# Writing out the last step of an attention loop, and storing each projected block once

## The chip, the cores and the metric

The kernel runs on one core of a Trainium2 chip. The metric is the device time of one execution in microseconds; the kernel before took 5323.51 us, the median of three runs that went from 5317.22 to 5327.42 us.

## The reference, cut to what matters

A two-layer hybrid network on `x` of shape (16, 512, 128) in float32: sixteen sequences of 512 tokens. Three of its stages are attentions with 16 heads of width 8:

```python
x = x + L0_attn_a(layernorm(x))   # causal, with a relative position bias per head
x = x + ffn(layernorm(x)); x = x + mamba(layernorm(x)); x = x + ffn(layernorm(x))
x = x + L1_attn_a(layernorm(x))   # not causal; keys and values from a latent of width 32
x = x + experts(layernorm(x))
x = x + L1_attn_b(layernorm(x))   # causal, q and k rotated by position
x = x + experts(layernorm(x))
# each attention:
scores = einsum('bhqd,bhkd->bhqk', q, k) / sqrt(8)  (+ bias, + mask)
out    = einsum('bhqk,bhkd->bhqd', softmax(scores), v) @ Wo
```

## The kernel before, in words

`program` runs the stages one after another; each is one or more phases, and at the end of a phase all engines meet in a barrier (`Phase.__exit__`, L58). An attention is a phase `project` and a phase `attend`; in the first one a short phase that lays out the relative bias stands between them. Below they are called a0 (bias, causal), a1 (not causal) and b1 (causal).

`project` goes over NB = 16 blocks of 512 tokens, one per sequence. TensorE, ScalarE, VectorE and GpSimd make q and k, each split into bf16 parts that add up to the float32 value, and v. SyncE (SP) then stores the block to DRAM: `store(n, u)` issues seven DMAs, six to the two `stack` tensors (L1068) and one to `values` (L1069), 1.75 MB in all. The DRAM tensors have NB + 1 blocks. After the sixteen blocks SP issues a seventeenth, `store(NB, ...)`, which writes the last block's data once more into place NB; at the end it waits for all stores.

`attend` works in groups of four heads: four groups to a sequence, 64 groups in all. Each group passes through a software pipeline whose stages are spread over steps. In step n the engines do, for the same instant of time:

- `scores_t` of group n (TensorE, L1302, with mask and bias matmuls L1320 and L1312): transposed scores into the three PSUM banks of `t_ps`; ScalarE turns each tile into `probs` with an exponential (L1428). In a0 VectorE first adds the bias to the first tile of each pair (L1476).
- `scores_s` of group n + 3 (TensorE, L1271) into the three banks of `s_ps`, of which VectorE takes the row maxima (`maxima`, L1462 when causal, L1465 when not). These are only for the shift of the softmax.
- `mt` of group n + 2 (TensorE, L1347), `shift_high` and `shift_low` (VectorE, L1488, L1494): the maxima are transposed, negated and split in two; SP stores them (`store_m`) and loads them back as extra rows of `t_q` (`load_t`).
- `pv` of group n - 1 (L1333), after which ScalarE copies `o_ps` to `o_sb` (L1414, once per group, near the start of a step), and `ot` of group n - 2 (L1354), with a reciprocal and a division on VectorE. Once per sequence come `bt` (L1360, with the copy `gather`) and `wo` (L1365, with the addition to x).

SP loads q and k of group n + 4 for the maxima (`load_s`) and those of group n + 1 for the transposed scores (`load_t`). Order on each engine is the order of the code; engines wait for each other on counting semaphores. `FIRST` and `USES` list the uses of the PSUM bank `misc`, so that each can wait for the one before by number.

The loop over sequences: b = 0 is written out; then TensorE, ScalarE and VectorE run `Fori(0, 15 // UNROLL)`, whose body holds UNROLL sequences. UNROLL is 1 in the causal attentions (12 tiles of a group divide by the ring of 3 banks) and 3 in a1 (16 tiles don't). So the loop has 15 turns of four steps in a0 and b1, and 5 turns of twelve steps in a1. No step asks whether group n + 3 still exists: in the last sequence (steps 60 to 63) the loads, scores and maxima of groups 64 to 67, a sequence past the end, are done on the extra DRAM block, and nothing uses them. After the loop a tail finishes `pv`, `ot`, `bt` and `wo` of the last groups.

Of the kernel before, what the change touches and what calls it, by code (L numbers as in the profile page):

```python
# [16 lines left out]
F32 = mybir.dt.float32  # L17
BF16 = mybir.dt.bfloat16
# [6 lines left out]
P = 128  # L25
NB = 16
T = 512
# [840 lines left out]
def project(core, x, stacks, v_dram, w):  # L868
# [10 lines left out]
    with core.phase() as ph:  # L879
# [180 lines left out]
        @block.sync  # L1060
        def _(sp):
            def store(n, u):
                for first, count in STEPS:
                    for s in range(2):
                        dst = stacks[s][n, :, first:first + count]
                        src = (parts[:, Q_PARTS[first], 0, u].unsqueeze(1).to_broadcast([P, count, T]) if s == 0
                               else parts[:, 0:count, 1, u])
                        sp.dma_start(dst, src).then_inc(stored[u], 16)  # L1068
                sp.dma_start(v_dram[n].rearrange("p c g d -> p (c g d)"), v_sb[:, u].rearrange("p c d -> p (c d)")  # L1069
                             ).then_inc(stored[u], 16)  # L1070

            for n in range(NB):
                sp.wait_ge(v_ready, n + 1)
                sp.wait_ge(middle_ready, 2 * n + 2)
                sp.wait_ge(low_ready, 2 * n + 2)
                store(n, n % PB)
            store(NB, (NB - 1) % PB)
            for u in range(PB):
                sp.wait_ge(stored[u], 16 * STORES * ((NB - 1 - u) // PB + 1 + (u == (NB - 1) % PB)))


def attend(core, x, stacks, v_dram, shift_dram, w, scale, causal, bias=None):
# [36 lines left out]
    with core.phase() as ph:  # L1119
# [38 lines left out]
        LEAD = 2  # L1158

        def use_no(b, g, what):  # L1160
            if isinstance(b, int) and b == 0:
                return LEAD + FIRST.index((g, what))
            return LEAD + len(FIRST) + len(USES) * (b - 1) + USES.index((g, what))

        def spread(b, k):

# [3 lines left out]
        def _(sp):  # L1170
# [43 lines left out]

            def step(b, g):
                n = 4 * b + g
                sp.wait_ge(s_mm, 2 * NTILE * (n + 2) + 2 * NTILE)
                load_s(b, g + 4)
                if not (isinstance(b, int) and n == 0):
                    sp.wait_ge(t_mm, USES_OF_GROUP * n)  # L1220
                sp.wait_ge(v_ready, n + 1 + 1)
                load_t(b, g + 1)
                store_m(use_no(b, g, "MT"), b, g + 2)

            for g in range(4):
                step(0, g)
            with sp.Fori(1, NB) as b:
                for g in range(4):
                    step(b, g)

            sp.wait_ge(s_loaded[0], 64 * 34)
            sp.wait_ge(s_loaded[1], 64 * 34)
            sp.wait_ge(t_loaded[0], 96 * 33)
            sp.wait_ge(t_loaded[1], 96 * 32)
            sp.wait_ge(v_loaded[0], 16 * 33)
            sp.wait_ge(m_stored[0], 16 * 33)
            sp.wait_ge(m_stored[1], 16 * 33)

        @block.gpsimd
        def _(pool):  # L1240
# [17 lines left out]
        def _(pe):  # L1258
# [114 lines left out]
            def step(b, v, g):  # L1373
                started = 4 * b + g if isinstance(b, int) else 99
                for pair, i in itertools.product(range(2), range(NTILE)):
                    at = NTILE * pair + i
                    scores_t(b, v, g, pair, i)
                    scores_s(b, v, g + AHEAD, pair, i)
                    if pv_pieces[at] and started >= 1:
                        pv(b, g - 1, *pv_pieces[at]) if g else pv(b - 1, 3, *pv_pieces[at])  # L1380
                    if at == misc_at["MT"]:
# [24 lines left out]
        def _(act):  # L1406
# [28 lines left out]
            for g in range(4):  # L1435
                step(0, 0, g)
            with act.Fori(0, (NB - 1) // UNROLL) as turn:
                for u in range(UNROLL):
                    for g in range(4):
                        step(UNROLL * turn + (1 + u), 1 + u, g)  # L1440
            last = use_no(NB, 0, "MT")
            evacuate(NB - 1, 2, use_no(NB - 1, 3, "OT"))
            evacuate(NB - 1, 3, last)

# [1 line left out]
        def _(dve):  # L1446
# [81 lines left out]
            def step(b, v, g):  # L1528
                started = 4 * b + g if isinstance(b, int) else 99
                for pair, i in itertools.product(range(2), range(NTILE)):  # L1530
                    at = NTILE * pair + i
                    if i in ADDED:
                        add_bias(b, v, g, pair, i)
                    maxima(b, v, g + AHEAD, pair, i)
                    if at == misc_at["MT"]:
                        shift_high(use_no(b, g, "MT"), b, g + 2)
                    if at == misc_at["MT"] + 1:
# [10 lines left out]
            for g in range(4):  # L1548
                step(0, 0, g)
            with dve.Fori(0, (NB - 1) // UNROLL) as turn:  # L1550
                for u in range(UNROLL):
                    for g in range(4):
                        step(UNROLL * turn + (1 + u), 1 + u, g)
            last = use_no(NB, 0, "MT")
            for k in (2, 3):
                sums_inverted(last + k - 2)
                divide(NB - 1, k)
# [639 lines left out]
def program(nc, a, out, phases=PHASES):  # L2197
    with ExitStack() as ctx:
# [13 lines left out]
        stacks = [nc.dram_tensor(f"stack_{s}", [NB + 1, P, PLACES, T], BF16).ap() for s in "qk"]  # L2212
        shift_dram = nc.dram_tensor("shifts", [NB + 1, HEADS, 4, SHIFT_ROWS, P], BF16).ap()
        v_dram = nc.dram_tensor("values", [NB + 1, P, 4, 4, 32], F32).ap()
# [184 lines left out]
```

## Time and profile before

| what | us |
|---|---|
| median of 3 runs | 5323.51 |
| the profiled execution | 5320.46 |
| its span, first to last instruction | 5318.7 |
| a0: project ends, attend runs | about 146, then 202 to 1004 |
| a1: project ends, attend runs | about 2636, then 2637 to 3440 |
| b1: project ends, attend runs | about 4133, then 4134 to 4756 |

Busy over the whole span: TensorE 78%, VectorE 67%, ScalarE 54%, GpSimd 30%. These are means over stages of different kinds; what the change touches lies in the three attentions, which take some 2250 us. Times in the rows below are microseconds from the start of the span.

### The profile page before, as it was taken

To read this page: it belongs to the slowest core of one execution; us is meant where nothing else is said; L and a number is where in the kernel's file an instruction comes from. 1 tells how busy PE (TensorE), PEld (TensorE's weight loads), DVE (VectorE), ACT (ScalarE), POOL (GpSimd) and SP (SyncE) were. 2 spreads that over 40 slices of the span, in tenths; PEclk is the share of its full clock that TensorE was granted. 3 is DMA by queue.
4 is the path that set the end of the run, shared out by engine and by line. 5 is a ranking of instruction groups with operands and counts; after the bars stand their busy time and mean duration, and the time that the engine had idled before them with its cause. 6 is when DMAs were issued, how large, how long until landed. Compare 5 with 4: busy or idle time off the path is not lost. (4 is left out here: it accounts for less than half of the span.)

```text
span 5318.7 us, 109649 instructions
## 1 busy us (share of the span) xinstructions
PE 4172.8 (78%) x31637; PEld 2106.4 (40%) x31638; DVE 3541.8 (67%) x8801; ACT 2850.0 (54%) x5331; POOL 1612.8 (30%) x1559
## 2 busy tenths in 40 slices
PE   6499999898667677778789999933987699983598
PEld 3144444552222222226222222323983244442497
DVE  3388888647899998984499999831116788873012
ACT  7255555676555555556667777721325466662232
POOL 3000000011777777741200000055536000006552
PEclk9699999999899998999889999966999799995799
DMA  7522222106100010000722222213665333321466
GB/s 257 150 73 72 74 76 72 33 0 216 42 26 26 26 36 28 26 13 2 244 73 74 78 76 75 72 38 123 214 189 209 108 95 96 98 77 46 142 212 191
DMA packets 546193, 502.03 MB, mean 94 GB/s; under 512 B 163774, under 2 KB 482911, under 8 KB 545788
## 3 DMA queue, kind: packets, MB, share of 16 engines
q1 hardware_dynamic: 527724, 460.95, 29.2%
q0 software_dynamic: 18160, 37.42, 2.1%
q8 instruction: 137, 2.24, 0.2%
q14 instruction: 172, 1.41, 0.1%
HBM read 330.57 MB, written 167.58 MB: 94 GB/s over the span
## 5 line engine op out<-in xcount | busy, mean ns | idle before, releaser
L1428 ACT ACTIVATE p_probs<-p_t_ps 128x512 f32<-128x512 f32 (+1 forms) x2304 | 1141.8, 551 | 680.9 <-PE p_t_ps L1320 243.8
L1963 PE MATMUL p_y_ps<-p_prod,c_ident 128*128 128x512 f32 x1024 | 554.5, 667 | 295.5 <-DVE p_prod L2148 290.9
L1333 PE MATMUL p_o_ps<-p_probs,p_v_st 128*32 128x256 f32 (+3 forms) x8704 | 727.0, 407 | 3.2 <-ACT p_o_sb L1414 2.9
L1465 DVE TENSOR_REDUCE p_row_max<-p_s_ps 128x1 f32<-128x512 f32 x1072 | 669.0, 680 | 71.9 <-PE p_s_ps L1271 55.6
L1254 POOL TENSOR_TENSOR p_v_st<-p_v_raw,p_ones 128x128 f32<-128x128 f32 x192 | 87.5, 456 | 2068.4 <-PE p_o_ps L1333 1946.9
L2097 POOL TENSOR_TENSOR p_dbx<-p_dtx,p_b_sb 128x512 f32<-128x512 f32 x512 | 632.4, 1267 | 113.2 <-ACT p_b_sb L1994 112.4
L2139 DVE TENSOR_TENSOR_SCAN p_state<-p_da,p_dbx 128x512 f32<-128x512 f32 x512 | 598.8, 1208 | 84.6 <-ACT p_da L2032 67.0
L1302 PE MATMUL p_t_ps<-p_t_q,p_t_k 50*128 50x512 bf16 (+3 forms) x3072 | 516.4, 336 | 147.6 <-ACT p_probs L1428 58.6
L1271 PE MATMUL p_s_ps<-p_s_k,p_s_q 48*128 48x512 bf16 (+3 forms) x3216 | 508.6, 340 | 146.8 <-DMA p_s_k<-stack_k 75.0
L1462 DVE CUSTOM_DVE_ANT_0 p_tried<-p_s_ps,p_s_bias 128x512 bf16<-128x512 f32 (+3 forms) x1072 | 470.5, 485 | 137.0 <-PE p_s_ps L1271 134.4
L1462 DVE CUSTOM_DVE_ANT_0 p_tried<-p_s_ps,c_mask_row 128x512 bf16<-128x512 f32 (+3 forms) x1072 | 470.5, 485 | 86.2 <-PE p_s_ps L1271 76.2
L791 DVE TENSOR_TENSOR p_y<-p_out_ps,p_raw 128x256 f32<-128x256 f32 x142 | 60.3, 425 | 581.3 <-PE p_out_ps L742 581.3
L1963 PEld LDWEIGHTS p_y_ps<-p_prod,c_ident 128*128 128x128 f32 x1024 | 188.7, 202 | 556.9 <-DVE p_prod L2148 478.3
L1994 ACT ACTIVATE p_b_sb<-p_b_ps 128x512 f32<-128x512 f32 x256 | 152.6, 596 | 430.2 <-PE p_b_ps L1932 419.4
L1302 PEld LDWEIGHTS p_t_ps<-p_t_q,p_t_k 50*128 50x128 bf16 x3072 | 149.1, 93 | 563.6 <-ACT p_probs L1428 361.5
L803 POOL DMA_INDIRECT weighed_rows<-p_y,p_raw x284 | 273.1, 962 | 296.9 <-DVE p_y L791 252.4
L2032 ACT ACTIVATE p_da<-p_dt,p_rate 128x512 f32<-128x512 f32 x512 | 337.4, 686 | 29.5 <-DVE p_state L2139 28.6
L773 ACT ACTIVATE p_hidden<-p_hid_ps 128x512 f32<-128x512 f32 x284 | 169.6, 597 | 316.0 <-PE p_hid_ps L731 313.7
L2148 DVE TENSOR_TENSOR p_prod<-p_state,p_c_ps 128x512 f32<-128x512 f32 x512 | 322.3, 670 | 0.0
L1312 PE MATMUL p_t_ps<-p_bias_parts,c_flip 64*128 64x384 bf16 (+2 forms) x4608 | 302.8, 269 | 0.0
L654 POOL DMA_INDIRECT routed_rows<-p_rows,p_index x256 | 249.2, 974 | 163.3 <-DVEq L599 86.5
L1333 PEld LDWEIGHTS p_o_ps<-p_probs,p_v_st 128*32 128x32 f32 x8704 | 174.7, 108 | 262.0 <-issue 245.4
(256 smaller groups left out, 6888.0 us busy)
## 6 DMA issues: line engine op xcount, KB each, us to landing
p_wb<-in_w SPq DMA_DIRECT2D x142, 512.0 KB
p_s_q<-stack_q SPq DMA_DIRECT2D x408, 96.0 KB
p_s_k<-stack_k SPq DMA_DIRECT2D x408, 96.0 KB
p_t_q<-stack_q SPq DMA_DIRECT2D x390, 96.0 KB
p_t_k<-stack_k SPq DMA_DIRECT2D x390, 96.0 KB
mamba_inputs<-p_out SPq DMA_DIRECT2D x17, 1536.0 KB, 5.7
p_inp<-mamba_inputs SPq DMA_DIRECT2D x17, 1536.0 KB
stack_q<-p_parts SPq DMA_DIRECT2D x51, 384.0 KB
```

The source lines that it names most:

```text
L1271: mm = pe.matmul(s_ps[:, banks[r], at:at + width], s_q[rows, g % 2, pair, c * P:(c + 1) * P], s_k[rows, g % 2, pair, 0:width], start=True, ...
L1302: mm = pe.matmul(out[r], t_k[rows, g % 2, pair, c * P:(c + 1) * P], t_q[rows, g % 2, pair, first:first + width], start=True, stop=not mask ...
L1312: mm = pe.matmul(out[r], bias["flip"][rows, k], bias["t"][q][rows, k, 2 * g + pair, first - c * P:first - c * P + width], start=False, sto ...
L1333: mm = pe.matmul(o_ps[32 * j:32 * j + 32, at:to], v_st[:, g % 2, c, j, :], probs[:, g % 2, j, place[c] + at - first:place[c] + to - first] ...
L1428: act.activation(exps, tile, ACT.Exp, scale=scale).then_inc(expd, 1)
L1462: read = dve.tensor_tensor_reduce(tried[:, slot, at:at + width], scores, over, 1.0, LOWEST, ALU.add, ALU.max, found)
L1465: read = dve.tensor_reduce(found, scores, X, ALU.max)
L1963: pe.matmul(y_ps[:, h], w["ident"], prod[:, k_slot(n, h, RS)], start=(n == 0), stop=(n == STATE - 1)).then_inc(acc_mm, 1)
L2032: act.activation(da[:, k_slot(n, h, RA)], dt[:, u, h], ACT.Exp, scale=rate[:, h, n:n + 1]).then_inc(da_ready, 1)
L2097: pool.tensor_tensor(dbx[:, k_slot(n, h)], dtx[:, u, h], b_sb[:, n % RB], ALU.mult).then_inc(dbx_ready, 1)
L2139: dve.tensor_tensor_scan(out=state[:, out], data0=da[:, k_slot(n, h, RA)], data1=dbx[:, s], initial=0.0, op0=ALU.mult, op1=ALU.add).then_i ...
L2148: dve.tensor_tensor(prod[:, s], state[:, s], c_ps[:, n % 2], ALU.mult).then_inc(prod_ready, 1)
```

## The change

`project`: the seventeenth store is gone, and with it its part of the final wait; the DRAM tensors have NB blocks instead of NB + 1.

`attend`: the last sequence is written out behind the loop, on TensorE, ScalarE, VectorE and SP (GpSimd keeps its loop over all 16). In the written-out copy `exists(b, k)` is known, and work on groups 64 and later is left out: `load_s` in all four steps, `scores_s` and `maxima` in steps 61 to 63, `mt` with its two shifts and its store in steps 62 and 63, `load_t` in step 63. For the loop to divide by UNROLL, it begins at sequence `FROM` = UNROLL: in a1 sequences 0, 1 and 2 are written out in front of it (before, only 0), the loop has 4 turns of three sequences instead of 5, and sequence 15 follows. In a0 and b1 the loop has 14 turns instead of 15.

```diff
-            store(NB, (NB - 1) % PB)
             for u in range(PB):
-                sp.wait_ge(stored[u], 16 * STORES * ((NB - 1 - u) // PB + 1 + (u == (NB - 1) % PB)))
+                sp.wait_ge(stored[u], 16 * STORES * ((NB - 1 - u) // PB + 1))
...
+    FROM, TO = UNROLL, NB - 1
+    GROUPS = 4 * NB
...
+        LAST = [use for use in USES if use not in ((2, "MT"), (3, "MT"))]
...
+        def exists(b, k):
+            return not isinstance(b, int) or 4 * b + k < GROUPS
...
             def step(b, g):
                 n = 4 * b + g
-                sp.wait_ge(s_mm, 2 * NTILE * (n + 2) + 2 * NTILE)
-                load_s(b, g + 4)
...
+                if exists(b, g + 4):
+                    sp.wait_ge(s_mm, 2 * NTILE * (n + 2) + 2 * NTILE)
+                    load_s(b, g + 4)
+                if exists(b, g + 1):
...
+                    load_t(b, g + 1)
+                if exists(b, g + 2):
+                    store_m(use_no(b, g, "MT"), b, g + 2)
...
-                    scores_s(b, v, g + AHEAD, pair, i)
+                    if exists(b, g + AHEAD):
+                        scores_s(b, v, g + AHEAD, pair, i)
...
-            for g in range(4):
-                step(0, 0, g)
-            with pe.Fori(0, (NB - 1) // UNROLL) as turn:
+            for b in range(FROM):
+                for g in range(4):
+                    step(b, b, g)
+            with pe.Fori(0, (TO - FROM) // UNROLL) as turn:
                 for u in range(UNROLL):
                     for g in range(4):
-                        step(UNROLL * turn + (1 + u), 1 + u, g)
-            last = use_no(NB, 0, "MT")
+                        step(UNROLL * turn + (FROM + u), FROM + u, g)
+            for g in range(4):
+                step(TO, TO, g)
+            last = END_USE
```

ScalarE and VectorE get the same loop as TensorE, `maxima` and the two shifts the same conditions; the numbers in `use_no` follow `LAST` in the last sequence.

## Rows read from the trace of the kernel before

**Rows 1.** SP's DMA issues at the end of project a0, then a1, then b1.

```profile
137.19 0.44 SPq L1069 DMA_DIRECT2D values<-p_v_sb  x1
142.52 0.45 SPq L1069 DMA_DIRECT2D values<-p_v_sb  x1
...
2627.67 0.45 SPq L1069 DMA_DIRECT2D values<-p_v_sb  x1
...
2632.97 0.45 SPq L1069 DMA_DIRECT2D values<-p_v_sb  x1
...
4124.89 0.46 SPq L1069 DMA_DIRECT2D values<-p_v_sb  x1
...
4130.23 0.44 SPq L1069 DMA_DIRECT2D values<-p_v_sb  x1
```

**Rows 2.** Window: from:to, length, PE, PEld, DVE, ACT, POOL busy, clock, DMA, GB/s.

```profile
2610.00:2634.00 24.00, 5.75 (x24) 2.86 (x23) 3.80 (x6) 7.95 (x15) 6.79 (x6) 0.66 1.00 345
```

**Rows 3.** GpSimd's first work in attend a1, with its idle time before.

```profile
2636.78 1.80 POOL L1242 MEMSET p_t_k<- 128x2048 bf16 x1 [16.57 <-POOLq L58]
```

**Rows 4.** Windows in a1: two ordinary steps; the same two around the first, last back-jump.

```profile
2806.07:2827.83 21.76, 20.45 (x186) 5.96 (x186) 21.27 (x42) 18.13 (x35) 0.91 (x2) 1.00 0.31 81
2850.95:2880.41 29.46, 23.86 (x186) 6.21 (x186) 21.64 (x42) 18.13 (x35) 0.91 (x2) 0.83 0.23 62
3277.24:3305.37 28.13, 22.60 (x186) 6.07 (x186) 21.46 (x42) 18.14 (x36) 0.91 (x2) 0.88 0.25 65
```

**Rows 5.** Weight loads behind the first back-jump; TensorE's waits, 2700 to 3430: total, times, longest.

```profile
2864.57 0.11 PEld L1302 LDWEIGHTS p_t_ps<-p_t_q,p_t_k 50*128 50x128 bf16 x2 [4.04 <-issue]
...
PE p_t_ps L1302 <- issue: 13.5, 4, 3.6
```

**Rows 6.** DMA queues between 340 and 990 (loop of a0): packets, MB, share.

```profile
q1 hardware_dynamic: 82028, 47.79, 27.3%
```

**Rows 7.** Windows over the first and the second turn of a0's loop.

```profile
284.53:332.53 48.00, 43.94 (x606) 22.45 (x604) 41.80 (x164) 24.96 (x54) 1.82 (x4) 1.00 0.28 77
332.53:380.00 47.47, 43.93 (x606) 22.37 (x604) 41.81 (x164) 24.96 (x53) 1.82 (x4) 1.00 0.27 72
```

**Rows 8.** Windows over steps 61 to 63 (eviction to eviction) of a0, a1, b1.

```profile
960.79:995.22 34.43, 32.21 (x445) 16.41 (x441) 30.09 (x120) 18.07 (x40) 0.91 (x2) 1.00 0.26 70
3395.33:3428.65 33.32, 31.60 (x281) 9.32 (x281) 32.10 (x62) 26.60 (x51) 0.91 (x2) 1.00 0.28 78
4719.62:4746.15 26.53, 24.36 (x325) 10.79 (x325) 23.76 (x107) 17.51 (x39) 0.91 (x2) 1.00 0.36 96
```

**Rows 9.** The same windows, instructions on `s_ps` alone: PE, PEld, DVE busy.

```profile
960.79:995.22 34.43, 5.88 (x46) 2.00 (x46) 20.73 (x48) 1.00 0.26 70
3395.33:3428.65 33.32, 8.89 (x46) 2.23 (x46) 29.08 (x48) 1.00 0.28 78
4719.62:4746.15 26.53, 5.92 (x46) 1.85 (x46) 20.39 (x47) 1.00 0.36 96
```

**Rows 10.** TensorE's weight loads in order, step 63 of a1, with idle before.

```profile
3418.61 0.10 PEld L1302 LDWEIGHTS p_t_ps<-p_t_q,p_t_k 50*128 50x128 bf16 x2 [0.54 <-ACT p_probs L1428]
3419.17 0.10 PEld L1271 LDWEIGHTS p_s_ps<-p_s_k,p_s_q 48*128 48x128 bf16 x2 [0.47 <-DVE p_row_max L1465]
3419.49 0.16 PEld L1333 LDWEIGHTS p_o_ps<-p_probs,p_v_st 128*32 128x32 f32 x8 [0.23 <-issue]
3420.49 0.09 PEld L1347 LDWEIGHTS p_misc<-c_ident,p_row_max 128*16 128x16 f32 x1 [0.84 <-DVE p_row_max L1465]
3420.69 0.10 PEld L1302 LDWEIGHTS p_t_ps<-p_t_q,p_t_k 50*128 50x128 bf16 x2
```

**Rows 11.** Weight loads' waits over steps 61 to 63 of a1: total, times, longest.

```profile
PEld p_t_ps L1302 <- ACT p_probs L1428: 7.3, 15, 1.0
...
PEld p_s_ps L1271 <- DVE p_row_max L1465: 4.2, 15, 0.5
PEld p_misc L1347 <- DVE p_row_max L1465: 2.5, 3, 0.8
```

More of the change, by code:

```diff
@@ L1162, in use_no @@
                 return LEAD + FIRST.index((g, what))
-            return LEAD + len(FIRST) + len(USES) * (b - 1) + USES.index((g, what))
+            uses = LAST if isinstance(b, int) and b == NB - 1 else USES
+            return LEAD + len(FIRST) + len(USES) * (b - 1) + uses.index((g, what))
+        def exists(b, k):
+            return not isinstance(b, int) or 4 * b + k < GROUPS
         def spread(b, k):
@@ L1216, in step @@
                 n = 4 * b + g
-                sp.wait_ge(s_mm, 2 * NTILE * (n + 2) + 2 * NTILE)
-                load_s(b, g + 4)
[L1219 to L1223, printed above, removed]
+                if exists(b, g + 4):
+                    sp.wait_ge(s_mm, 2 * NTILE * (n + 2) + 2 * NTILE)
+                    load_s(b, g + 4)
+                if exists(b, g + 1):
+                    if not (isinstance(b, int) and n == 0):
+                        sp.wait_ge(t_mm, USES_OF_GROUP * n)
+                    sp.wait_ge(v_ready, n + 1 + 1)
+                    load_t(b, g + 1)
+                if exists(b, g + 2):
+                    store_m(use_no(b, g, "MT"), b, g + 2)
             for g in range(4):
                 step(0, g)
-            with sp.Fori(1, NB) as b:
+            with sp.Fori(1, TO) as b:
                 for g in range(4):
                     step(b, g)
[L1231 to L1237, printed above, removed]
+            for g in range(4):
+                step(TO, g)
+            for u in range(2):
+                sp.wait_ge(s_loaded[u], 64 * (GROUPS // 2))
+                sp.wait_ge(t_loaded[u], 96 * (GROUPS // 2))
+                sp.wait_ge(v_loaded[u], 16 * (GROUPS // 2))
+                sp.wait_ge(m_stored[u], 16 * (GROUPS // 2))
         @block.gpsimd
@@ L1388, in step @@
                         bt(use_no(b, g, "BT"))
[L1390 to L1392 removed]
+            for b in range(FROM):
+                for g in range(4):
+                    step(b, b, g)
+            with pe.Fori(0, (TO - FROM) // UNROLL) as turn:
                 for u in range(UNROLL):
                     for g in range(4):
[L1395 to L1396 removed]
+                        step(UNROLL * turn + (FROM + u), FROM + u, g)
+            for g in range(4):
+                step(TO, TO, g)
+            last = END_USE
             for piece in pv_pieces:
@@ L1433, in step @@
                         evacuate(b, g - 2, before) if g >= 2 else evacuate(b - 1, g + 2, before)
-            for g in range(4):
-                step(0, 0, g)
-            with act.Fori(0, (NB - 1) // UNROLL) as turn:
+            for b in range(FROM):
+                for g in range(4):
+                    step(b, b, g)
+            with act.Fori(0, (TO - FROM) // UNROLL) as turn:
                 for u in range(UNROLL):
                     for g in range(4):
-                        step(UNROLL * turn + (1 + u), 1 + u, g)
-            last = use_no(NB, 0, "MT")
+                        step(UNROLL * turn + (FROM + u), FROM + u, g)
+            for g in range(4):
+                step(TO, TO, g)
+            last = END_USE
             evacuate(NB - 1, 2, use_no(NB - 1, 3, "OT"))
@@ L1533, in step @@
                         add_bias(b, v, g, pair, i)
-                    maxima(b, v, g + AHEAD, pair, i)
-                    if at == misc_at["MT"]:
+                    if exists(b, g + AHEAD):
+                        maxima(b, v, g + AHEAD, pair, i)
+                    if at == misc_at["MT"] and exists(b, g + 2):
                         shift_high(use_no(b, g, "MT"), b, g + 2)
-                    if at == misc_at["MT"] + 1:
+                    if at == misc_at["MT"] + 1 and exists(b, g + 2):
                         shift_low(b, g + 2)
@@ L1546, in step @@
                         gather(use_no(b, g, "BT"))
-            for g in range(4):
-                step(0, 0, g)
-            with dve.Fori(0, (NB - 1) // UNROLL) as turn:
+            for b in range(FROM):
+                for g in range(4):
+                    step(b, b, g)
+            with dve.Fori(0, (TO - FROM) // UNROLL) as turn:
                 for u in range(UNROLL):
                     for g in range(4):
-                        step(UNROLL * turn + (1 + u), 1 + u, g)
-            last = use_no(NB, 0, "MT")
+                        step(UNROLL * turn + (FROM + u), FROM + u, g)
+            for g in range(4):
+                step(TO, TO, g)
+            last = END_USE
             for k in (2, 3):
@@ L2211, in program @@
         load_x(core, a["x"], x, (ident, a["ident"]), loads)
-        stacks = [nc.dram_tensor(f"stack_{s}", [NB + 1, P, PLACES, T], BF16).ap() for s in "qk"]
-        shift_dram = nc.dram_tensor("shifts", [NB + 1, HEADS, 4, SHIFT_ROWS, P], BF16).ap()
-        v_dram = nc.dram_tensor("values", [NB + 1, P, 4, 4, 32], F32).ap()
+        stacks = [nc.dram_tensor(f"stack_{s}", [NB, P, PLACES, T], BF16).ap() for s in "qk"]
+        shift_dram = nc.dram_tensor("shifts", [NB, HEADS, 4, SHIFT_ROWS, P], BF16).ap()
+        v_dram = nc.dram_tensor("values", [NB, P, 4, 4, 32], F32).ap()
         masks = {name: small[name][:, :, :] for name in ("ident16", "mask_t")}
```

3 lines of the change are left out of this document (2 added, 1 removed).

## The prediction

> **What bounds the kernel now.** The page's busy shares are means over unlike stages, so I read only the places that the change touches, by the order of the phases.
>
> First SP's own timeline at the end of each projection. The reader is to see that the block's last DMA, the one to `values`, follows that of the block before at a fixed distance: 5.33 us in a0, 5.30 in a1, 5.34 in b1 [rows 1], with SP issuing all the while. In the last 24 us of project a1 the DMA engines are busy all the time at 345 GB/s [rows 2], and a block of 1.83 million bytes (seven stores, 1.75 MB) needs 5.3 us at that rate: SP and the DMA engines are equally the bound. The computing engines are long done: GpSimd, the last of them, sat idle for 16.57 us before attend a1 [rows 3]. So the end of a projection is its stores, the seventeenth of them last.
>
> Then windows over stretches of attend. In steps 61 to 63 (one eviction of `o_ps` to the next) TensorE is busy 32.21 of 34.43 us in a0, 31.60 of 33.32 in a1 and 24.36 of 26.53 in b1, VectorE 30.09, 32.10 and 23.76, ScalarE 18.07, 26.60 and 17.51 [rows 8]. VectorE's 32.10 of 33.32 make it a1's bound; in a0 and b1 TensorE and VectorE alternate.
>
> Last, a1's loop. Two ordinary steps take 21.76 us; the same two around a back-jump of the loop take 29.46 the first time and 28.13 the last [rows 4]. TensorE stands for 4.04 us with nothing to wait for that the profile shows, and such stops come four times in a1, once per back-jump of a loop of five turns [rows 5]. The mean granted clock over the pair drops to 0.83 and 0.88 [rows 4]: some of TensorE's time behind the stop runs at 1.2 instead of 2.4 GHz. That is a surcharge of 7.70 and 6.37 us, 7.0 in the mean.
>
> **Part 1: the seventeenth stores.** Seven DMA issues and 1.83 million bytes go from each of three projections. Nothing takes their place: the last real block was made before, and its own stores stay where they are, so the phase ends one block's distance earlier. 5.33 + 5.30 + 5.34 = 16.0 us [rows 1]. In a0 the next phase begins with loads on the same queue, which then start earlier by the same amount. TensorE's idle time at the start of the next phase is shorter by 5 us, too little against the 16 us and more that it stands there to count on any gain from the clock; I take none. Bounds: if SP had to wait for the last block, up to 1 us of each could be missing; 15 to 16.
>
> **Part 2: one back-jump less in a1.** Five turns have four back-jumps, four turns have three. The two added written-out sequences cost what the first turn cost, since that too was met going straight on. So one surcharge goes: 7.0 us, bounds 6.4 and 7.7 [rows 4]. In a0 and b1 there is nothing of the kind to win: between 340 and 990 us, fourteen turns of a0's loop, the only DMA queue with traffic is that of data [rows 6], no instruction is fetched, and the turns have no surcharge.
>
> The Trainium skill ("Runtime: NRT & Kernel Launch", Instruction fetch mechanics) says that TensorE holds 2048 instructions, filled in blocks of 256 in order, and that a taken branch to a place outside the current two-page window stops the engine for a fetch. The stop of rows 5 is such a one. But by the two-page window a0's loop, with 606 matmuls a turn [rows 7], would stop at every turn as well, and by that the change would win a surcharge more in each of a0 and b1, 14 us together; rows 6 speaks against it, and the measurement decides.
>
> **Part 3: the lighter last steps.** Removed in each attention: `scores_s` of three groups, 48 matmuls and 48 maxima. On TensorE the profile puts 5.88, 8.89 and 5.92 us to them, on VectorE 20.73, 29.08 and 20.39 [rows 9]. Two transpositions with their shifts, 23 loads (16 in `load_s`, 7 in `load_t`) and 2 stores of SP go too; nothing on another engine that is left waits for them, so these alone are worth nothing.
>
> VectorE is then nearly free. What is late next? The upper bound is the busiest engine of what is left: TensorE 32.21 - 5.88 = 26.3 us in a0 (8.1 us to win), ScalarE 26.60 in a1 (6.7), TensorE 24.36 - 5.92 = 18.4 in b1 (8.1) [rows 8, 9]: 22.9 us in all. The lower bound is nothing: in front of a tile, TensorE often waits until ScalarE has read a bank of the three, 15 times in a1's 24 tiles for 7.3 us together [rows 11], and where that wait ends last a missing `scores_s` only makes it longer.
>
> Between the two I walk a1's step 63. From one `scores_t` to the next are 2.08 us: in it 0.47 us wait for a maximum, 0.32 us `scores_s`, 1.00 us `pv`, and a transposition after another wait of 0.84 [rows 10] (which begins while `pv` is still running). Without the scores `pv` could come 0.2 us after the tile and the next tile 1.0 us behind; but ScalarE has two exponentials and the eviction to get through, 0.52 us each (26.60 us for 51 [rows 8]), about 1.5 us from tile to tile. Gain 0.6. Three more of the eight gaps are set by TensorE's queue (behind `ot`, before the `bt` or `wo`, and one with a long wait for maxima); each loses the 0.32 us of the scores and little more. The other four are set by the exponentials and give nothing. That makes 1.4 us a step, 4.2 for a1, 0.6 of its bound; the waits for maxima, 4.2 + 2.5 us [rows 11], could not give more than that, since they overlap with waits for banks. In a0 and b1 the tiles are longer chains (bias or mask matmuls ahead of the exponential), and by the same walk three gaps of six give 1.1 to 1.5 us a step: 4.4 and 3.4 us, about half of the bounds. Sum 12.0 us.
>
> **Part 4: what is added.** The last sequence is code met for the first time. What that costs is in a0's first turn against its second: 48.00 against 47.47 us [rows 7], 0.5 us. Three times at most this is 1.5; I take 1.0. That more is left to fetch is otherwise hidden, as it is in the first turns. No wait is added.
>
> **The sum.** 16.0 + 7.0 + 12.0 - 1.0 = 34.0 us. The profiled execution took 5320.5 us (its span of 5318.7 and 1.8 around it), which gives 5286.5. The median of the runs is 3.0 us above the profiled one; I forecast 5289.5.
>
> **The rivals.**
>
> A. *The exponentials' chain sets the last steps alone.* Then VectorE's relief and TensorE's are both waited away and part 3 is 0 to 1 us: 5301. For it: 15 of 24 tiles wait for a bank [rows 11]. Against: a1's VectorE is busy 32.10 of 33.32 us [rows 8], which no exponential explains.
>
> B. *The steps run to the bound of the busiest engine.* Part 3 is 22.9: 5278.6. For it: in a1 ScalarE has 6.7 us of idle time that VectorE's pace explains. Against: three banks leave little slack to fill TensorE in a0 and b1.
>
> C. *Leaving the loop costs a refill.* Before, the loop was left into a short tail; now a whole sequence at full pace follows, in a0 some 1200 instructions of TensorE [rows 7]. If the exit stops TensorE as a back-jump does, each attention pays up to 7.0 us: 5310.5. Against: the exit is the way straight on, and a1's twelve steps of one turn run on without a stop [rows 4, 5].
>
> D. *A loop is no longer held: slower.* The written-out code of a0 and a1 moves b1's loop against the blocks in which instructions are fetched. If it then is not held any more, each of its 13 back-jumps stops the engines as in a1: 13 x 7.0 = 91 us, against 34 won: 5380. It decides from the fifth or so back-jump with a stop. Against: a0's turn has 606 matmuls and is held [rows 6, 7], b1's turn has fewer (325 in three steps against 445 [rows 8]), which leaves room for any position.
>
> E. *The extra work was hidden, or the two-page rule holds.* The first would leave 5323, but rows 1 to 3 show nothing that hides the stores; the second gives 5275.5.
>
> **How the numbers follow.** The forecast has 62 in 100, A 12, B 10, C 10, D 4, E 2. The forecast's own range is 5283 to 5297. For 8 in 10 I add the near parts of A and B and half of C: 5275 to 5306. A measurement of this kernel can tell from no change about 0.2%, 10.6 us: below 5312.9 is faster. All but D and half of E lie there; with something for a mishap within a few of the back-jumps: faster 0.93, same 0.03, slower 0.04.
>
> **What would show it.** Part 1: between the last `values` store and the next phase 3 to 4 us as now, and GpSimd idle for 11 instead of 16.6 us before attend a1. Part 2: three stops of 3.6 us in a1 instead of four. Part 3: windows over steps 61 to 63 of about 30.0 us in a0, 29.1 in a1 and 23.1 in b1; if they are 34.4, 33.3 and 26.5, A is right, if 26.3, 26.6 and 18.4, B. Part 4 and C: TensorE idle with "issue" as the cause at the start of step 60 would mean C. D: traffic in the instruction queue all through b1's loop. The prediction is wrong as a whole if any step outside the three attentions moves by more than a few microseconds, since I take none of them to change.

## The result, and the profile after

The changed kernel took 5295.91 us in the median of 6 runs (5288.13 to 5297.26), the kernel before 5320.57 (5317.08 to 5327.42), run in turn on one chip: ratio 0.9949, 95% interval 0.9936 to 0.9962. That is 27 us less by the ratio and 24.7 by the medians. Forecast were 5289.5 and a range of 5275 to 5306, so the kernel is faster, by half a percent, and the time is in the range; the gain is 7 to 9 us smaller than the 34.0 that the sum had. The profiled execution took 5290.52 us, its span 5288.7, against 5318.7: 30.0 less.

On two of the chips that the experiments ran on, one phase of each of the two expert stages, outside of all that is changed, takes some 200 us where it took 222 here. So below a time stands only beside the kernel before of the same chip, as a ratio, and stages are compared by their own lengths.

First SP's issues at the end of project a0, then a1, then b1, which answer to [rows 1], in the changed kernel's trace (start, length, what).

```profile
130.63 0.45 SPq L1069 DMA_DIRECT2D values<-p_v_sb  x1
...
135.96 0.46 SPq L1069 DMA_DIRECT2D values<-p_v_sb  x1
...
2618.35 0.45 SPq L1069 DMA_DIRECT2D values<-p_v_sb  x1
...
2623.65 0.46 SPq L1069 DMA_DIRECT2D values<-p_v_sb  x1
...
4096.78 0.45 SPq L1069 DMA_DIRECT2D values<-p_v_sb  x1
4102.09 0.44 SPq L1069 DMA_DIRECT2D values<-p_v_sb  x1
```

The distance of the blocks is what it was, 5.33, 5.30 and 5.31 us; there is one block less. GpSimd shows it from the other side: its first work in attend a1 comes after 11.23 us of idle time, not 16.57 [rows 3]. The forecast had said 11.

```profile
2627.43 1.80 POOL L1253 MEMSET p_t_k<- 128x2048 bf16 x1 [11.23 <-POOLq L58]
```

Next windows in a1 (columns as in [rows 2]): two ordinary steps, then the same two around each of the three back-jumps, and TensorE's idle time for which the profile has no cause.

```profile
2796.79:2818.56 21.77, 20.49 (x186) 6.08 (x186) 21.27 (x41) 18.14 (x35) 0.91 (x2) 1.00 0.31 82
2931.46:2958.12 26.66, 21.88 (x186) 6.04 (x186) 21.46 (x42) 18.14 (x36) 0.91 (x2) 0.94 0.28 69
3071.02:3097.93 26.91, 22.44 (x186) 6.07 (x186) 21.45 (x42) 18.14 (x35) 0.91 (x2) 0.87 0.27 69
3210.83:3238.01 27.18, 22.31 (x186) 6.08 (x186) 21.46 (x42) 18.14 (x35) 0.91 (x2) 0.87 0.26 67
```

```profile
PE p_t_ps L1313 <- issue: 10.4, 3, 3.7
```

Three stops where there were four [rows 5], each about as long as before. But the surcharges are 4.9, 5.1 and 5.4 us, not 6.4 to 7.7 [rows 4]: all three ended up cheaper than any of the four, and the reader sees the first with a mean clock of 0.94 against 0.83.

Last, windows over steps 61 to 63 of a0, a1 and b1, against [rows 8].

```profile
954.78:987.80 33.02, 29.18 (x397) 15.67 (x393) 9.90 (x20) 18.06 (x39) 0.92 (x2) 1.00 0.09 24
3372.68:3403.06 30.38, 25.50 (x233) 8.09 (x233) 3.65 (x10) 26.59 (x51) 0.92 (x2) 1.00 0.11 28
4692.34:4716.38 24.04, 20.67 (x277) 9.66 (x277) 3.59 (x10) 17.53 (x39) 0.92 (x2) 1.00 0.14 35
```

48 matmuls and VectorE's 20 to 29 us are gone, and the stretches are shorter by only 1.4, 2.9 and 2.5 us. TensorE's busy time fell by 3.0, 6.1 and 3.7 us, not by the 5.9, 8.9 and 5.9 that [rows 9] put to the scores. The matmuls that are left last as long as before (those of `pv` 391 ns in the mean before and after in a0, those of `scores_t` 386 and 382 ns in a1). The scores' matmuls had overlapped with their neighbours: leave them and the transpositions of the maxima out of the count in the trace of the kernel before, and TensorE is still busy for 29.6, 25.9 and 21.0 us of the three windows.

### The profile page after: what moved, and what is told of

The parts are those of the page before. It is cut to its first block and busy times, and to the rows that moved or that the text cites. A ratio compares the mean times of both kernels' runs of the same rounds, so it can differ in the third digit from the quotient of the medians.

```text
span 5288.7 us, 107821 instructions
## 1 busy us (share of the span) xinstructions
PE 4154.8 (79%) x31487; PEld 2105.7 (40%) x31488; DVE 3470.7 (66%) x8549; ACT 2851.1 (54%) x5331; POOL 1615.8 (31%) x1559
## 3 DMA queue, kind: packets, MB, share of 16 engines
q8 instruction: 142, 2.33, 0.2%
q14 instruction: 167, 1.37, 0.1%
## 5 line engine op out<-in xcount | busy, mean ns | idle before, releaser
L1483 DVE TENSOR_REDUCE p_row_max<-p_s_ps 128x1 f32<-128x512 f32 x1024 | 638.7, 679 | 55.5 <-PE p_s_ps L1282 49.5
L1282 PE MATMUL p_s_ps<-p_s_k,p_s_q 48*128 48x512 bf16 (+3 forms) x3072 | 485.3, 340 | 131.5 <-DMA p_s_k<-stack_k 64.6
L1480 DVE CUSTOM_DVE_ANT_0 p_tried<-p_s_ps,p_s_bias 128x512 bf16<-128x512 f32 (+3 forms) x1024 | 449.5, 485 | 133.7 <-PE p_s_ps L1282 131.3
L1480 DVE CUSTOM_DVE_ANT_0 p_tried<-p_s_ps,c_mask_row 128x512 bf16<-128x512 f32 (+3 forms) x1024 | 449.4, 485 | 79.3 <-PE p_s_ps L1282 69.6
```

Source lines behind the costliest of these rows:

```text
L1282: mm = pe.matmul(s_ps[:, banks[r], at:at + width], s_q[rows, g % 2, pair, c * P:(c + 1) * P], s_k[rows, g % 2, pair, 0:width], start=True, ...
L1480: read = dve.tensor_tensor_reduce(tried[:, slot, at:at + width], scores, over, 1.0, LOWEST, ALU.add, ALU.max, found)
L1483: read = dve.tensor_reduce(found, scores, X, ALU.max)
```

## The experiments

**The first four**: where do the 27 us come from, part by part? They ran on one chip, beside the kernel before at 5271.64. A number such as 0.9961 is a run's ratio to the kernel before of its chip, with its 95% interval in brackets.

`again` is the changed kernel unaltered.

> The changed kernel itself once more, as the base for the three beside it. If what lies outside the three attentions and differed between the first two profiles (the mamba scan's phase 3.7 us longer, one layer norm 1.6 shorter) is only the spread of executions, it comes out otherwise here; if the code's new place in memory makes it, the scan's phase is 1046.6 us again and not 1042.9. Time: 5294, within 4.

It gave 0.9961 [0.9947, 0.9975], 20.6 us by this ratio; its interval and that of the first chip, around 0.9949, overlap from 0.9947 to 0.9962. The phases that the change touches are as long as in the first profile within 2.7 us. The Mamba scan, a long phase between a0 and a1 whose code is not changed, takes 1046.2 us again, against 1042.9 in the first profile of the kernel before, so its growth belongs to the changed kernel; the layer norm is back at the 33.7 us of the kernel before, so its 1.6 us were spread.

`store17` brings the seventeenth stores back.

```diff
+            store(NB, (NB - 1) % PB)
...
-        v_dram = nc.dram_tensor("values", [NB, P, 4, 4, 32], F32).ap()
+        v_dram = nc.dram_tensor("values", [NB + 1, P, 4, 4, 32], F32).ap()
```

> The changed kernel with the seventeenth store of each projection put back (and its DRAM block). Theory: the stores are the end of each projection, so each of the three phases is one block's distance longer, 5.3 us by the issue rows, 17.3 together by the phases of the two profiles: 16 to 17.5 us over the changed kernel. Rival (part of the 17.3 came from executions that happened to differ): 12 or less.

0.9984 [0.9974, 0.9993]: 14.7 us slower than `again` by the medians, between the rival's 12 and the 16 to 17.5 of the theory. The phases decide it: the three projections together are 16.2 us longer than in `again`, and the scan, which the edit doesn't touch, is 2.6 shorter. The projections are back at 110.7, 118.6 and 145.0 us, the lengths of the kernel before (110.7, 118.6, 144.6); over nine profiles without the stores they are 104.9, 113.3 and 139.2 in the mean. Part 1 stands alone in this edit, so it is shown: 5.4 us each.

`extra` is `store17` with all work on groups 64 and later kept in the written-out last sequence: the control flow is the changed one, the work that of before.

```diff
-        LAST = [use for use in USES if use not in ((2, "MT"), (3, "MT"))]
+        LAST = USES
...
-            return not isinstance(b, int) or 4 * b + k < GROUPS
+            return True
```

> The run before, and the last sequence written out with all the work on groups 64 and later kept: loads, scores, maxima, transpositions. It needs the seventeenth store, so it is to be compared with that run. Theory (the chain of exponentials and PSUM banks takes over where the scores go): the work is worth 1.4 us in a0, 2.9 in a1, 2.1 in b1, 6.4 together, and the windows over steps 61 to 63 are 34.4, 33.3 and 26.5 us again. Rival (the relief is the 12 us of my forecast, and code met for the first time took 6 of it back): 12 us over the run before, and steps 60 to 63 longer than 34.4, 33.3 and 26.5 plus an ordinary step 60.

0.9978 [0.9968, 0.9988], so by the medians the additional work costs nothing, and neither theory nor rival is met; it comes out 2.5 us ahead of `store17`. The windows say otherwise: steps 61 to 63 take 34.47, 33.42 and 26.72 us here against 33.02, 30.39 and 24.04 in `store17`. So the work costs 7.2 us, near the theory's 6.4, and step 60, the first of the written-out ones, is no longer than in `store17` (11.44, 10.86 and 8.73 us against 11.45, 10.86 and 8.87). As much and more comes back elsewhere: the Mamba scan, a phase that none of these edits touches, is 1032.2 us long here and 1043.5 in `store17`. That is what the last group of runs is about.

`noloop` writes all 16 sequences of a1 out on TensorE, ScalarE and VectorE, so no back-jump is left in it.

```diff
-    FROM, TO = UNROLL, NB - 1
+    FROM, TO = UNROLL if causal else NB - 1, NB - 1
...
-            with pe.Fori(0, (TO - FROM) // UNROLL) as turn:
+            if TO > FROM:
+                with pe.Fori(0, (TO - FROM) // UNROLL) as turn:
```

> The changed kernel with all sixteen sequences of a1 written out on TensorE, ScalarE and VectorE (SP and GpSimd keep their loops): no back-jump in a1. Theory (each back-jump stops TensorE for 4 us and the lower clock behind it costs 1 to 4 more, straight code costs nothing): three surcharges of 4.9 to 5.4 us go, attend a1 is 15.4 us shorter, 5279. Rival 1 (the loop's size in memory is the cost, and longer straight code stops as well): within 3 us of the changed kernel. Rival 2 (my price of 7.0 each holds in most executions): 21 us shorter.

0.9924 [0.991, 0.9937], 15.3 us faster than `again`. From the first eviction to the last, a1 takes 698.1 us against 714.3: 16.2, and `again`'s three surcharges add up to 17.4; the rest is the 0.1 us by which each of the twelve sequences is longer when written out. The window that answers to the second back-jump, in the trace of `noloop`:

```profile
3071.58:3093.34 21.76, 20.75 (x186) 6.27 (x186) 21.16 (x41) 18.13 (x35) 0.91 (x2) 1.00 0.31 81
```

An ordinary pair at full clock. So code met for the first time runs at the loop's pace (a sequence takes 45.0 us here, 44.9 in the loop), and a back-jump costs all of its surcharge. For this the prediction had an estimate only. What `noloop` takes away is the loop of three engines, and all three stand at the jump: in the kernel before, the first register operation behind the first jump comes at 2862.99 us on ScalarE, 2863.89 on VectorE and 2864.13 on TensorE, 2.65, 3.33 and 3.93 us after the branch. TensorE is last there by 0.24 us; in `again` VectorE is, at all three jumps (by 1.1 to 1.5 us). So the surcharge is shown to be the jump's, but not to be TensorE's alone.

**Three banks or the engines**: `sixbanks` lets the transposed tiles of groups 61 to 63 go round six PSUM banks, the three of `s_ps` too, which nobody else uses then. If the chain through the exponentials and three banks is what holds the last steps (rival A in part), they must get shorter; if not, they stay as they are.

```diff
+            q = (USES_OF_GROUP * (g - 1) + 2 * NTILE * pair + 2 * i + r) % (2 * RING)
+            if q < RING:
+                return t_ps, (USES_OF_GROUP * (4 * v + 1) + q) % RING
+            return s_ps, q - RING
```

> The changed kernel, in which the transposed tiles of groups 61 to 63 go round six PSUM banks, the three of t_ps and the three of s_ps that no scores need any more. Theory (with the scores gone, TensorE waits for the exponential, or the added bias, of the tile before the last, since there are three banks; that swallowed most of the relief): the windows over steps 61 to 63, now 33.0 us in a0, 30.4 in a1 and 24.0 in b1, fall towards TensorE's own 26.3 and 18.4 us in a0 and b1 and ScalarE's 26.6 in a1; I expect 28.5, 27.5 and 20.5, 11 us together. Rival (TensorE's queue order, the pieces of pv and the transpositions set the steps): within 1 us of 33.0, 30.4 and 24.0.

0.9947 [0.993, 0.9963], on a chip where the changed kernel with some idle instructions (`pad_pe`, below) gave 0.9952: too near for the medians. The windows of `sixbanks`, steps 61 to 63 in a0, a1 and b1:

```profile
957.06:988.35 31.29, 27.72 (x389) 14.45 (x387) 9.90 (x20) 18.05 (x39) 0.92 (x2) 1.00 0.10 24
3377.14:3404.61 27.47, 24.32 (x233) 7.53 (x233) 3.65 (x10) 25.25 (x51) 0.91 (x2) 1.00 0.12 31
4692.37:4714.76 22.39, 19.70 (x277) 9.20 (x277) 3.59 (x10) 17.52 (x40) 0.92 (x2) 1.00 0.15 37
```

1.7, 2.9 and 1.7 us shorter, 6.3 together where I expected 11. In a1 the 27.5 us came as expected, and ScalarE is now the busiest engine, 25.25 of 27.47 us; the banks had held back 2.9 us. In a0 and b1 my aims, 28.5 and 20.5 us, were set by the 26.3 and 18.4 us that the forecast had called TensorE's own, and those were too low (29.6 and 21.0, see above). The weight loads' waits in a1 (total, times, longest), first of the changed kernel, then of `sixbanks`, show how (PEld is TensorE's weight load, the first instruction of a matmul):

```profile
PEld p_t_ps L1313 <- ACT p_probs L1443: 12.7, 17, 1.0
```

```profile
PEld p_t_ps L1332 <- ACT p_probs L1463: 4.5, 7, 0.9
...
PEld p_o_ps L1363 <- ACT p_probs L1463: 3.7, 3, 1.6
```

The wait for a bank was 7.3 us while the scores were there [rows 11], grew to 12.7 once they were gone, and falls to 4.5 with six banks (and 0.8 for tiles in the other three). In the changed kernel's a1 an undisturbed gap from tile to tile is 1.14 us:

```profile
3387.50 0.10 PEld L1313 LDWEIGHTS p_t_ps<-p_t_q,p_t_k 50*128 50x128 bf16 x2 [0.17 <-issue]
3387.82 0.16 PEld L1344 LDWEIGHTS p_o_ps<-p_probs,p_v_st 128*32 128x32 f32 x8 [0.23 <-issue]
3388.64 0.12 PEld L1313 LDWEIGHTS p_t_ps<-p_t_q,p_t_k 50*128 50x128 bf16 x2 [0.66 <-ACT p_probs L1443]
```

That is two exponentials of 0.52 us and the way through the semaphore. The 1.5 us of the prediction's walk counted the eviction into every gap; but the long gaps (1.97 us with a `wo` in it) stay long.

**Both together**: `both` is `noloop` with `sixbanks`, on the chip of `sixbanks`.

> No loop in a1 and six banks in the last three steps. If the two gains don't touch each other: 15.4 us (three surcharges of 4.9 to 5.4 us; the run without the loop measured 0.9924 of the kernel before against 0.9961) and 11 us below the changed kernel, a ratio to the kernel before of 0.990.

0.9906 [0.9888, 0.9924]: 24.8 us faster than `sixbanks`, 28.9 than `pad_pe` (below), which does the changed kernel's work. The last steps' windows are those of `sixbanks` within 0.01 us and a1's surcharges are nothing: the two gains add.

**The scan phase.** In the first profile the Mamba scan, between a0 and a1, had grown from 1042.9 to 1046.6 us, and its code is the same. On VectorE something new is to be seen at each of its loop's five back-jumps. The timeline of VectorE around the third, changed kernel:

```profile
1844.12 2.45 DVE L2161 TENSOR_TENSOR_SCAN p_state<-p_da,p_dbx 128x512 f32<-128x512 f32 x2 [0.19 <-POOL p_dbx L2119]
1846.49 1.26 DVE L2170 TENSOR_TENSOR p_prod<-p_state,p_c_ps 128x512 f32<-128x512 f32 x2
1849.97 1.22 DVE L2161 TENSOR_TENSOR_SCAN p_state<-p_da,p_dbx 128x512 f32<-128x512 f32 x1 [2.22 <-ACT p_da L2054]
1852.38 1.22 DVE L2161 TENSOR_TENSOR_SCAN p_state<-p_da,p_dbx 128x512 f32<-128x512 f32 x1 [1.19 <-ACT p_da L2054]
1853.52 1.26 DVE L2177 TENSOR_TENSOR p_gated<-p_y_ps,p_inp 128x512 f32<-128x512 f32 x2
```

VectorE stops at the jump, does one scan, and stops again before its twin. The idle time is put down to ScalarE's `da`, but the `da` of the second scan was done at 1849.2, over 3 us before that scan. Between the two scans VectorE's sequencer stands still: two register operations of its own that follow each other lie 2.2 us apart there, 2.0 to 2.2 at all five jumps, and the `da` for which the second of them has to wait was done 2.9 us or more before the scan at each. The kernel before has the first stop only (two scans in one row, x2). My theory: the attentions' longer code has moved the scan loop, so that it now starts a few instructions ahead of the end of a fetched block; the jump fetches that block, and at once the next. To test it without touching the scan, instructions that only count a semaphore up were put at the end of project a0, where the engines wait for SP's stores: `pad_dve` has 120 on VectorE, `pad_pe` 105 on TensorE.

```diff
+            for _ in range(120 if not latent and not rotary else 0):
+                dve.sem_inc(filler, 1)
```

> The changed kernel with 120 increments of an unused semaphore at the end of VectorE's part of project a0, where VectorE idles for over 15 us: nothing but the place of VectorE's later code in memory moves, by as much as in the run that kept the extra work. Theory P (the mamba scan's time hangs on where a loop's code lies against the blocks in which it is fetched, on VectorE): the scan's phase is 1032 us as in that run, not 1046, and the kernel 10 us faster. Rival (it hangs on the phase of the clock or on chance): 1043 to 1050.

> The same on TensorE, with 105 increments, the other engine whose code in front of the mamba scan was longer in that run. Theory P for TensorE: the scan's phase is 1032 us. Rival: 1043 to 1050.

`pad_dve` gave 0.992 [0.9904, 0.9937], `pad_pe` 0.9952 [0.9936, 0.9969]. In `pad_dve` the two scans follow each other without a second stop and the phase takes 1037.0 us; in `pad_pe` the second stops are there and it takes 1050.4. So it is VectorE's code whose place matters, and 120 instructions that do nothing make the kernel 18 us faster than `pad_pe` by the medians. The scan phase has 13 of that; the rest lies scattered over other phases, 1 to 3 us in each.

`pad8` is the same with 8 instead of 120; `before_moved` is the kernel before with 80; `before_twin` is the kernel before in one more profile. They ran with `all` beside a kernel before of 5275.29. Counting VectorE's instructions modulo 128, I expected 8 to be enough and 80 to bring the second stops into the kernel before.

> The changed kernel with 8 increments of an unused semaphore on VectorE, at its idle end of project a0. In the changed kernel VectorE stops twice at each of the five back-jumps of the mamba scan's loop, 2.8 us at the jump and 2.0 to 2.3 us a few instructions later; in the kernel before, and where 120 increments moved the code, only the first stop is there. Theory (the loop begins a few instructions before the end of a block of instructions, so that the next block is needed at once): 8 instructions more put its begin behind the block's edge, the second stop is gone, the scan's phase is 1032 to 1037 us instead of 1043 to 1050, and the kernel 8 to 14 us faster, a ratio to the kernel before of 0.992 to 0.993. Rival (the 120 instructions helped otherwise, by the phase of the clock or the time of a later stage): second stops as before, 0.995.

> The kernel before, nothing changed but 80 such increments on VectorE at the same place. VectorE's code in front of the scan was 176 instructions longer there than in the changed kernel; with 80 more it lies, by blocks of 128, where the changed kernel has it. Theory: second stops of 2.0 to 2.3 us appear at the five back-jumps, and the kernel gets 5 to 10 us slower than it was, a ratio of 1.001 to 1.002. Rival: no second stops, 1.000.

> The kernel before once more, for the spread of its phases. Back-jumps of a1: four, with surcharges between 4.9 and 7.7 us, as the stretch of lower clock behind each comes out at 3.4, 6.8 or 10.2 us; scan's phase 1043 us within 4 and no second stop; steps 61 to 63 the same to 0.1 us.

`pad8` gave 0.992 [0.9907, 0.9934], no second stops, scan 1039.3 us. Here the same spot in its trace:

```profile
1845.12 2.45 DVE L2164 TENSOR_TENSOR_SCAN p_state<-p_da,p_dbx 128x512 f32<-128x512 f32 x2 [0.18 <-POOL p_dbx L2122]
1847.49 1.26 DVE L2173 TENSOR_TENSOR p_prod<-p_state,p_c_ps 128x512 f32<-128x512 f32 x2
1850.74 2.34 DVE L2164 TENSOR_TENSOR_SCAN p_state<-p_da,p_dbx 128x512 f32<-128x512 f32 x2 [1.99 <-POOL p_dbx L2122]
```

One stop, then both scans. The instruction queue tells the same, here in 9 us behind this third jump in the changed kernel, in `pad8` and in `pad_dve` (packets, MB, share):

```profile
q14 instruction: 3, 0.02, 1.1%
```

```profile
q14 instruction: 2, 0.02, 0.6%
```

```profile
q14 instruction: 3, 0.02, 0.9%
```

In all 14 profiles two packets of 8 KB on this queue start about 1.0 to 1.3 and 3.4 to 3.8 us behind each back-jump. VectorE goes on 2.7 to 3.1 us behind the jump. Where it has second stops, they end at 5.1 to 5.6 us, 1.7 to 1.9 us after the start of the second packet, and a third packet follows; in `pad8`, `all` and the three profiles with the code of before there are only two packets and no stop. `pad_dve` and `extra` are a third case: they have the three packets, and VectorE's sequencer stands still for 1.5 to 1.7 us until 5.2 to 5.5 us as well, but seven recorded instructions later, while the engine is busy with the second scan. So in these the second fetch is hidden and not gone. An edge that 8 more instructions take out of the way and 120 more push a few instructions further back fits blocks of 128 instructions.

`before_moved` was a miss: no second stops, and 0.9981 [0.9972, 0.999], faster instead of slower. `before_twin` has none either; its one execution took 5272.92 us. So 8 instructions are enough to take the second stops away (shown twice, here and in `all`), while my sum for where a block begins in the kernel before is wrong or incomplete, and that stays open. That unrecorded instructions shift it is a guess. Of the 14 profiles the seven with second stops have a scan of 1043.5 to 1050.4 us, 1047.1 in the mean, the seven without 1032.2 to 1042.9, mean 1037.3. One profile alone would not tell: the two of the same kernel before have 1042.9 and 1036.0. The difference of 9.8 us is nearly five times 2.1.

`all` is `noloop`, `sixbanks` and the 8 instructions together.

> No loop in a1, six banks in the last three steps, and VectorE's code moved by 8 instructions. If the three add up: the run of the first two had a ratio of 0.9906, the third is worth 8 to 14 us: 0.988 to 0.989.

0.9878 [0.9863, 0.9893], 5209.96 us beside 5275.29: the best version, 65 us faster than the kernel before and 26 faster than `pad8`.

## Why the prediction was right, and where it was not

| step | forecast | first profile | over the runs |
|---|---|---|---|
| Part 1, stores | -16.0 | -17.3 | -16.3 |
| Part 2, back-jumps in a1 | -7.0 | -12.6 | -12.4 |
| Part 3, last steps | -12.0 | -6.8 | -6.8 |
| Part 4, fresh code (step 60) | +1.0 | +0.6 | +0.5 |
| Mamba scan | 0 | +3.7 | +7.2 |

"Over the runs" are means over the profiles that have the part in question against the three of the kernels with the work of before (`before`, `before_twin`, `before_moved`); for part 2 those are eight profiles with three surcharges (14.4 to 19.5 us together, mean 16.8) against 28.1, 34.2 and 25.4 for four, and for the scan the seven with second stops (1047.1) against 1039.9. The last column gives -27.8, where the ratio says 27; a handful of differences of 1 to 2 us in other phases, of both signs, isn't explained. The first profile's column adds up to -32.4 for a difference of 30.0.

**Part 1** was right in mechanism and size: the end of a projection is its stores, and they follow at a fixed distance. The 17.3 us of the first profile and the 16.3 of all lie a little above its bounds of 15 to 16.

**Part 2** was right in mechanism, and the term was mis-sized. One surcharge of 7.3 us went, as forecast, but the three left cost 5.6 us in the mean instead of 7.3, another 5 us. TensorE's stop is the same (4.15, 4.11, 3.59 and 3.97 us from weight load to weight load before, 3.98, 3.88 and 4.28 after). What shrank is what follows: the granted clock is at 1.2 GHz for 10.2, 6.8, 10.2 and 6.8 us before, for 3.4, 6.8 and 6.8 after. How long this stretch is differs from run to run of equal code (6.8 to 10.2 us in `before`, 10.2 to 13.7 in `before_twin`), and with it the price of a jump: over all profiles with the loop it is 4.4 to 4.9 us with a stretch of 3.4 us, 5.1 to 6.6 with 6.8, 6.8 to 7.9 with 10.2 and 8.5 to 9.3 with 13.7. So one profile couldn't give the price closer than to some 2 us, and the forecast's bounds of 6.4 and 7.7 were the two jumps that it had looked at. With 6.8 us the changed kernels still pay less, 5.4 in the mean against 6.2; with 10.2 us they pay the same, 7.4 against 7.5. Why they pay less there, and what sets the length of the stretch, no run tells.

**Part 3** is the step that failed in size: 6.8 instead of 12.0. By attention: a0 1.4 for 4.4, a1 2.9 for 4.2, b1 2.5 for 3.4. In a1 and b1 the walk was off by a quarter to a third (and its own terms, 0.6 and three times 0.32, make 1.6 us a step and not 1.4). Six banks show what rules in a1: the banks, until ScalarE does; that the banks hold b1 as well is shown for the 1.7 us that it gained. In a0 the walk was carried over from a1 by analogy and gave three times too much. There the waits for a bank are few. The weight loads' waits in a0's window of the changed kernel:

```profile
PEld p_t_ps L1313 <- issue: 7.6, 13, 1.5
...
PEld p_t_ps L1313 <- ACT p_probs L1443: 1.6, 3, 0.5
```

TensorE stands ahead of a tile 13 times for something that these rows don't name, and three times for a bank; `sixbanks` won 1.7 us there all the same. The rows of its matmuls in the same window name one thing more:

```profile
PE p_t_ps L1313 <- DVE p_probs L1494: 2.4, 2, 1.2
```

Twice a tile waits until VectorE has added the bias, which frees a bank in a0. What else holds a0's steps stays open. Nor does rival B's bound hold as an amount: TensorE's busy time in a0 was to fall to 26.3 us and fell to 29.2. The scores' 5.88 us were subtracted as if nothing ran beside them. With the 29.6 and 21.0 us that the trace of the kernel before has without them, B's part 3 would have been 4.9, 6.7 and 5.5 us, 17.1 and not 22.9. `extra` against `store17` confirms the 6.8 from the other side (7.2). So A's chain of exponentials and banks took back more than half of a1's 6.7 us (2.9 won with three banks, 5.9 with six), but part 3 as a whole is not the 0 to 1 us that A gives.

**Part 4, rivals C and E**: no stop at a loop's exit. Step 60 takes 11.45, 10.85 and 8.87 us against 11.37, 10.77 and 8.48, 0.6 in all, and in `pad_dve`, `pad8` and `noloop` b1's takes 8.72. Rival C's surcharge of up to 7.0 us each is refuted. Rival E's hidden stores are too: by the phases of `store17` they cost 16.2 us.

**Rival D and the last sentence.** No loop of the attentions lost its hold: the instruction queues are silent in a0's loop, and b1's turns keep their time. But the condition under which the prediction called itself wrong as a whole, that a step outside the attentions moves by more than a few microseconds, was met: the scan grew by 3.7 us in the first profile and by 7.2 in the mean. As a forecast of the stages it was wrong there, though the total held. The mechanism of D, code that moves against the blocks in which it is fetched, did happen, at a place that I hadn't looked at, with 2.1 us instead of 7.0 a jump, on VectorE instead of TensorE. The error was to search for moved code only inside of the phases that the diff touches. The Trainium skill ("Runtime: NRT & Kernel Launch", Instruction fetch mechanics) has the rule that a taken branch out of what is held fetches its target page; what is seen here is 5 stops of about 2.8 us on VectorE in all kernels, and five further ones in half of the profiles. Its two-page window, taken for TensorE as well, would have had a0's loop on TensorE stop at each turn, which the rows spoke against and which did not happen.

The 5 us too few of part 2 and the 5 us too many of part 3 offset, so that the miss of 7 us in the total is that of the scan. That the time lies in the range is owed to that luck as much as to the argument.

## What to carry to other kernels

A phase that ends in stores issued one after another ends earlier by one block's distance if a block goes (here 5.3 us, 5.4 measured), however idle the computing engines are. Removing work from a stage gives what the next chain allows: count the buffers that the next engine must free (here three PSUM banks and exponentials of 0.52 us) before taking the busy time as a bound, don't subtract a group's busy time from TensorE's where its matmuls overlap with others, and don't carry one stage's walk over to another. A price that hangs on the clock behind a stop wants more than one profile. In a long kernel with loops, a longer or shorter program ahead of a loop can change the loop's time; for differences as small as these (0.2 to 0.5%) compare two versions by stages, and try a few idle instructions ahead of a loop before believing a difference of the whole.

## What the runs showed of the hardware

- The loop of a1 costs 4.4 to 9.3 us at each back-jump: a stop of some 4 us on TensorE (and of 2.5 to 4.5 on ScalarE and VectorE, which run the same loop), and TensorE's granted clock at 1.2 GHz for 3.4 to 13.7 us behind it. Written out, a sequence takes 45.0 us against 44.9, and 16.2 of 17.4 us are saved.
- Which loops stop goes with their length in these traces. From one back-jump to the next the traces record 1312 instructions of TensorE in a0 and 989 in b1, and no stop; in a1 they record 2589, and a stop at each. On VectorE it is 250 and 216 without a stop, 397 (a1) and 508 (the scan) with one.
- The page's queues in the changed kernel: instructions come in packets of 16 KB on one queue (2.33 MB by 142) and of 8 KB on the other (1.37 MB by 167). During a1 the written-out version moves fewer of both than the loop does (49 and 21 against 56 and 46 from 2700 to 3400 us), so fetching straight on is no burden.

```profile
q8 instruction: 142, 2.33, 0.2%
q14 instruction: 167, 1.37, 0.1%
```

- A second stop of 2.0 to 2.3 us on VectorE right behind a back-jump came and went with the place of the code, by 8 instructions that ran some 1200 us ahead of the phase: 5 stops and 10 us of 5290. It ends 1.7 to 1.9 us after the start of the second 8 KB packet, and the same wait costs little where an instruction of over 1 us is under way.
- The kernel before itself gains 0.2% by 80 idle instructions on VectorE (0.9981 [0.9972, 0.999]); a1's surcharges are 25.4 us there against 28.1 and 34.2 in the two profiles of the kernel before itself, and a0's attend 801.8 against 803.0 and 803.7.
